# Expert results added to the output rows by accumulating scatters instead of a scratch array and a summing phase

## The chip, the cores and the metric

The kernel runs on one core of a Trainium2 chip. The metric is the device time of one execution in microseconds (us). The profile is one further execution with the hardware profiler on; times inside it count from the start of its span.

## What is computed

The input is 8192 tokens of 128 channels. A graph layer and causal attention come first. Then each token is routed to its two best experts of eight, and this is the part that the change touches. Cut to that part, the reference is:

```python
probs = jax.nn.softmax(flat @ router_w.T, axis=-1)
tp, ti = jax.lax.top_k(probs, TOPK)                      # TOPK = 2, NE = 8
tp = tp / (jnp.sum(tp, axis=-1, keepdims=True) + 1e-09)
weights = jnp.sum(tp[..., None] * jax.nn.one_hot(ti, NE, dtype=flat.dtype), axis=1)
out = jnp.zeros_like(flat)
for e in range(NE):
    hh = jax.nn.silu(flat @ w1[e].T) * (flat @ w3[e].T)
    out = out + weights[:, e:e + 1] * (hh @ w2[e].T)
return x + out.reshape(Bx, Tx, Cx)
```

The result row of a token is thus the residual row plus two weighted expert rows.

## The kernel before

The kernel has three stages, `graph_stage`, `attention_stage` and `expert_stage`, with a barrier of all engines between them. Each stage writes one program per engine by hand, and semaphores order the engines; there is no scheduler. The names in the profile are `PE` (matrix engine), `DVE` (vector), `ACT` (scalar), `POOL` (GpSimd) and `SP` (the engine that only issues transfers).

`attention_stage` ends by leaving the residual of all tokens in on-chip memory (`keep["attended"]`, 128 partitions by 8192) and by scattering every token twice into the DRAM array `scratch_slots`, once per chosen expert, so that each expert's tokens stand together. A slot row holds 128 channels, the routing weight, and a target row number. The target numbers come from POOL's `count_up(target...)`; in the kernel before, token and choice `k` give a row of the scratch array `scratch_parts` (16384 rows: two per token).

`expert_stage` works on groups of 512 slots of one expert. There are `GROUPS` = 39 of them, the greatest number that can occur; groups that are not needed read empty slots, whose target is out of range, so that the scatter writes nothing for them. For each group g:

- SP loads the 512 slot rows into `x_rows` (six buffers).
- PE turns them (`ps_x`), ACT and DVE split them into a high and a low half-precision part (`x_hi`, `x_lo`), PE multiplies by `w1`, `w3` and, one group behind, `w2`; ACT and DVE work on the hidden values between.
- ACT copies the product (`moeT`), PE turns it back (`ps_y`), and DVE, in `scale_parts(g)`, casts the target numbers (`y_index`, L1860) and multiplies by the routing weights (`y_rows`, L1862, semaphore `y_scaled`). `y_rows` and `y_index` have two buffers, so `scale_parts(g)` first waits until the scatter of group g - 2 has landed (`y_scattered`).
- POOL waits for `y_scaled` and issues four indirect transfers of 128 rows each (L1744) into `scratch_parts`.

Behind the last group comes the summing phase. SP waits for all scatters and loads `scratch_parts` in 16 blocks of two parts (L1719, four buffers `parts`), DVE adds the two parts (L1893), POOL adds the residual (L1752), and ACT stores the block to `out` (L1800).

At the start of the stage ACT makes the high halves of the three weight arrays (`w_hi`, L1760), and goes on with `split_tokens(0)`, which writes `x_hi` of the first group (L1766). PE's first product of the stage waits for that.

Of the kernel before, what the change touches and what calls it, by code (L numbers as in the profile page):

```python
# [18 lines left out]
F32 = mybir.dt.float32  # L19
# [6 lines left out]
P = 128  # L26
C = 128
# [633 lines left out]
def attention_stage(nc, NB, dram, keep):  # L661
# [164 lines left out]
    with ExitStack() as ctx:  # L826
# [157 lines left out]
        def _(pool):  # L984
# [72 lines left out]
            for k in range(TOPK):  # L1057
                count_up(target[:, :, :, k], [[BT, NB], [1, SUB]], base=k * N, per_partition=SUB)
            for q in range(PAIRS):
# [545 lines left out]
def expert_stage(nc, NB, dram, keep):  # L1605
# [15 lines left out]
    BUFFERS = 2  # L1621
    PB = 4
    LAST = NB - 1
    TOKEN_SCALE, WEIGHT_SCALE, HIDDEN_SCALE = 2.0 ** 4, 2.0 ** 6, 2.0 ** 4
    with ExitStack() as ctx:
# [26 lines left out]
        y_index = sb("y_index", [P, 2, SUB], mybir.dt.uint32)  # L1652
        parts = sb("parts", [P, PB, TOPK, BT])
        residual = keep["attended"]
# [30 lines left out]
        y_scattered = [sem(f"y_scattered{n}") for n in range(BUFFERS)]  # L1685
        parts_loaded = [sem(f"parts_loaded{n}") for n in range(PB)]
        parts_added = sem("parts_added")
        result_ready = sem("result_ready")
        result_stored = [sem(f"result_stored{n}") for n in range(PB)]
        block = ctx.enter_context(nc.Block())  # L1690
# [4 lines left out]
        @block.sync  # L1695
        def _(sp):
            sp.dma_start(ln2[:], dram["ln2"]).then_inc(small_in, 16)
            for n, name in enumerate(WEIGHTS):
                sp.dma_start(exact[name][:], dram[name]).then_inc(weights_in[n], 16)

            sp.wait_ge(last_scattered, 16 * SUB * TOPK)
            sp.wait_ge(table_ready, 2)
            for g in range(GROUPS):
                if g >= XB:
                    sp.wait_ge(x_turned, g - XB + 1)
                    sp.wait_ge(y_scaled, g - XB + 1)
                start = sp.value_load(start_index[0:1, g:g + 1], min_val=0, max_val=NE * N)
                sp.dma_start(x_rows[:, g % XB], dram["slots"][ds(start, GROUP), :].rearrange("(p s) c -> p s c", s=SUB)
                             ).then_inc(x_loaded[g % XB], 16)

            for n in range(BUFFERS):
                sp.wait_ge(y_scattered[n], 16 * SUB * len(range(n, GROUPS, BUFFERS)))
            for T in range(NB):
                n = T % PB
                if T >= PB:
                    sp.wait_ge(result_stored[n], 16 * (T // PB))
                for k in range(TOPK):
                    at = (k * NB + T) * BT
                    sp.dma_start(parts[:, n, k, :], dram["parts"][at:at + BT, :].rearrange(  # L1719
                        "(p s) c -> p (s c)", s=SUB)).then_inc(parts_loaded[n], 16)  # L1720

        @block.gpsimd
        def _(pool):
# [17 lines left out]
            for g in range(GROUPS):  # L1741
                pool.wait_ge(y_scaled, g + 1)
                for s in range(SUB):
                    pool.indirect_dma_start(  # L1744
                        dram["parts"], bass.IndirectOffsetOnAxis(y_index[:, g % BUFFERS, s:s + 1], 0),
                        y_rows[:, g % BUFFERS, s, :], None, bounds_check=TOPK * N - 1, oob_is_err=False
                    ).then_inc(y_scattered[g % BUFFERS], 16)

            for T in range(NB):
                pool.wait_ge(parts_added, T + 1)  # L1750
                result = parts[:, T % PB, 0, :]
                nc.gpsimd.tensor_tensor(result, result, residual[:, T * BT:(T + 1) * BT], ALU.add).then_inc(result_ready, 1)  # L1752

        @block.scalar
        def _(act):
            act.wait_ge(small_in, 16)
            nc.scalar.mul(ln2_scaled[:], ln2[:], TOKEN_SCALE).then_inc(ln2_ready, 1)
            for n, name in enumerate(WEIGHTS):
                act.wait_ge(weights_in[n], 16)
                nc.scalar.mul(w_hi[name][:], exact[name][:], WEIGHT_SCALE).then_inc(weight_hi_ready, 1)  # L1760
            act.wait_ge(ln2_ready, 1)
            def split_tokens(g):
# [33 lines left out]
            copy_moe(GROUPS - 1)  # L1796

            for T in range(NB):
                act.wait_ge(result_ready, T + 1)
                act.dma_start(dram["out"].rearrange("(b s p) c -> b p s c", s=SUB, p=P)[T], split(parts[:, T % PB, 0, :])  # L1800
                              ).then_inc(result_stored[T % PB], 16)
            for n in range(PB):
                act.wait_ge(result_stored[n], 16 * (NB // PB))

        @block.vector
        def _(dve):
# [82 lines left out]

            for T in range(NB):  # L1890
                n = T % PB
                dve.wait_ge(parts_loaded[n], 16 * TOPK * (T // PB + 1))
                nc.vector.tensor_tensor(parts[:, n, 0, :], parts[:, n, 0, :], parts[:, n, 1, :], ALU.add  # L1893
                                        ).then_inc(parts_added, 1)

        @block.tensor
# [70 lines left out]
def program(nc, N, dram):  # L1967
    NB = N // BT
    for name, shape, dt in (("x1", (NB, P, SUB, C), F32), ("z", (NB, P, SUB, C), F32),
                            ("lower", (NB, P, BT), F32), ("q_hi", (P, N), F16), ("q_lo", (P, N), F16), ("k_hi", (P, N), F16),  # L1970
                            ("slots", (NE * N + GROUP, ROW), F32), ("parts", (TOPK * N, C), F32)):
        dram[name] = nc.dram_tensor(f"scratch_{name}", shape, dt, kind="Internal").ap()
# [70 lines left out]
```

## Time and profile before

| | us |
|---|---|
| median of three timed runs | 3520.46 (3517.39 to 3522.1) |
| profiled execution, its own time | 3524.27 |
| span in the profile | 3522.5 |
| mean granted TensorE clock | 0.943 of full speed |
| start of `expert_stage` in the span | 3164.2 |
| first scatter of results issued | 3214.1 |
| last of the 156 scatters issued | 3471.1 |

The span is shorter than the execution's own time by what lies around it, 1.8 us. The three stages follow each other, so shares over the whole span say little of the last stage; the rows below are of that stage unless their line says otherwise.

### The profile page before, as it was taken

To read this page: it belongs to the slowest core of one execution; us is meant where nothing else is said; L and a number is where in the kernel's file an instruction comes from. 1 tells how busy PE (TensorE), PEld (TensorE's weight loads), DVE (VectorE), ACT (ScalarE), POOL (GpSimd) and SP (SyncE) were. 2 spreads that over 40 slices of the span, in tenths; PEclk is the share of its full clock that TensorE was granted. 3 is DMA by queue.
4 is the path that set the end of the run, shared out by engine and by line. 5 is a ranking of instruction groups with operands and counts; after the bars stand their busy time and mean duration, and the time that the engine had idled before them with its cause. 6 is when DMAs were issued, how large, how long until landed. Compare 5 with 4: busy or idle time off the path is not lost. (4 is left out here: it accounts for less than half of the span.)

```text
span 3522.5 us, 56503 instructions
## 1 busy us (share of the span) xinstructions
PE 3085.2 (88%) x22241; PEld 1353.5 (38%) x22241; DVE 2554.2 (73%) x2736; ACT 1423.8 (40%) x2843; POOL 1728.2 (49%) x1113
## 2 busy tenths in 40 slices
PE   2678889899989987998999999999999999957992
PEld 1334434344434432433433333333333333324661
DVE  8888887675554455779878977877987898616773
ACT  0000000000000003666666666666666666745661
POOL 0000000000321113776888699877699869763665
PEclk9778999999999997999999999999999999988996
DMA  9898876678667944440000000000000000002224
GB/s 376 349 391 366 349 308 267 282 296 302 254 261 292 359 155 167 160 164 13 29 18 18 7 24 17 11 8 7 7 17 18 11 2 17 9 26 93 74 74 154
DMA packets 157501, 506.75 MB, mean 144 GB/s; under 512 B 20081, under 2 KB 66298, under 8 KB 112326
## 3 DMA queue, kind: packets, MB, share of 16 engines
q1 hardware_dynamic: 111400, 448.58, 32.9%
q10 hardware_dynamic: 33024, 31.47, 2.7%
q0 software_dynamic: 12816, 23.11, 2.0%
q8 instruction: 179, 2.93, 0.3%
q14 instruction: 82, 0.67, 0.1%
HBM read 426.31 MB, written 75.37 MB: 142 GB/s over the span
## 5 line engine op out<-in xcount | busy, mean ns | idle before, releaser
L1223 DVE TENSOR_REDUCE unit_max<-ps_max 128x2 f32<-128x1024 f32 (+2 forms) x1088 | 1225.9, 1171 | 297.4 <-PE ps_max L1452 254.1
L998 POOL TENSOR_TENSOR chunk_sum<-chunk_sum,probs 128x1024 f32<-128x1024 f32 x480 | 1132.3, 2359 | 287.8 <-ACT probs L1093 277.1
L1093 ACT ACTIVATE probs<-ps_ring 128x512 f32<-128x512 f32 x2112 | 1089.8, 596 | 440.2 <-PE ps_ring L1471 408.1
L566 PE MATMUL ps_gather<-ring,keep_attended 128*128 128x512 f32 x1688 | 789.8, 625 | 140.1 <-DMA ring<-in_adj 121.4
L1471 PE MATMUL ps_ring<-q_stack,keep_shared 97*128 97x512 f16 x2112 | 673.9, 385 | 27.7 <-ACT probs L1093 22.2
L1486 PE MATMUL ps_acc<-probs,keep_shared 128*32 128x256 f32 (+1 forms) x8448 | 566.8, 386 | 0.0
L566 PEld LDWEIGHTS ps_gather<-ring,keep_attended 128*128 128x128 f32 x1688 | 332.6, 202 | 541.7 <-issue 541.7
L367 DVE TENSOR_TENSOR work<-work,ring 128x2048 f32<-128x2048 f32 x195 | 446.6, 2290 | 34.5 <-DMA ring<-in_adj 30.7
L342 POOL DMA_DIRECT2D scratch_lower<-lower x13 | 7.3, 560 | 805.0 <-ACT lower L484 805.0
L1452 PE MATMUL ps_max<-k_heads,q_heads 32*128 32x512 f16 (+3 forms) x2176 | 276.0, 378 | 69.9 <-DVE unit_max L1223 48.5
L1495 PE MATMUL ps_acc<-probs,keep_ones_heads 128*32 128x256 f32 (+1 forms) x4224 | 327.9, 380 | 0.0
L1471 PEld LDWEIGHTS ps_ring<-q_stack,keep_shared 97*128 97x128 f16 x2112 | 163.5, 98 | 407.7 <-ACT probs L1093 252.0
L1486 PEld LDWEIGHTS ps_acc<-probs,keep_shared 128*32 128x32 f32 x8448 | 222.2, 110 | 244.4 <-issue 121.8
L1744 POOL DMA_INDIRECT scratch_parts<-moe_y_rows,moe_y_index x156 | 168.5, 1080 | 126.5 <-DVE moe_y_rows L1862 87.9
L1452 PEld LDWEIGHTS ps_max<-k_heads,q_heads 32*128 32x128 f16 x2176 | 73.4, 91 | 339.0 <-DVE unit_max L1223 195.5
L350 POOL TENSOR_TENSOR q_lo<-rotated,q_hi 128x512 f16<-128x512 f32 x16 | 18.4, 1151 | 337.0 <-DVEq L460 337.0
L1495 PEld LDWEIGHTS ps_acc<-probs,keep_ones_heads 128*32 128x32 f32 x4224 | 138.0, 111 | 87.7 <-issue 4.1
L566 PE MATMUL ps_gather<-keep_shared,keep_attended 128*128 128x512 f32 x360 | 160.9, 603 | 2.5 <-DVE keep_attended L376 2.5
L367 DVE TENSOR_TENSOR work<-work,keep_shared 128x2048 f32<-128x2048 f32 x45 | 103.1, 2292 | 79.4 <-DMA keep_shared<-in_adj 78.8
L1038 POOL DMA_INDIRECT scratch_slots<-batch_rows,keep_slot_index x120 | 118.8, 990 | 38.1 <-POOL chunk_sum L998 26.0
L473 ACT ACTIVATE root_degree<-ps_degrees 128x4 f32<-128x4 f32 x16 | 2.8, 173 | 324.3 <-PE ps_degrees L593 324.3
L1878 DVE SCALAR_TENSOR_TENSOR moe_hidden<-moe_ps_up,moe_gate 114x512 f32<-114x512 f32 (+1 forms) x117 | 80.9, 691 | 64.0 <-ACT moe_gate L1786 62.8
(243 smaller groups left out, 2667.5 us busy)
## 6 DMA issues: line engine op xcount, KB each, us to landing
ring<-in_adj SPq DMA_DIRECT2D x302, 1024.0 KB, 13.9
keep_shared<-in_adj SPq DMA_DIRECT2D x45, 1024.0 KB, 10.8
scratch_slots<-empty_rows SPq DMA_DIRECT2D x16, 2080.0 KB, 14.3
moe_x_rows<-scratch_slots SPq DMA_DIRECT2D x39, 260.0 KB, 2.7
moe_parts<-scratch_parts SPq DMA_DIRECT2D x32, 256.0 KB, 4.2
x_in<-in_x SPq DMA_DIRECT2D x16, 256.0 KB, 13.3
x_in<-in_x ACTq DMA_DIRECT2D x16, 256.0 KB, 7.5
work<-in_cos ACTq DMA_DIRECT2D x16, 256.0 KB, 4.1
```

What stands on the lines that cost most here:

```text
L367: add = nc.vector.tensor_tensor(total, total, tile_of[g, False], ALU.add)
L566: last = nc.tensor.matmul(bank[:], support[:, s * SUB + c, :], tile_of[g, is_again][:, c * BT:(c + 1) * BT], start=(first and c == 0), sto ...
L998: steps.then(nc.gpsimd.tensor_tensor(totals, totals, weights, ALU.add))
L1038: pool.indirect_dma_start(dram["slots"], bass.IndirectOffsetOnAxis(slot_index[:, at, k:k + 1], 0), rows_of(b)[:, at // SUB, at % SUB, k, : ...
L1093: nc.scalar.activation(probs[:, q % SLOTS, i, kv, :, lo:], halves(bank)[:, :, lo:], ACT.Exp, scale=SCALE).then_inc(ring_read, 1)
L1223: nc.vector.tensor_reduce(unit_max[:, half % 2, heads, s % 2, unit], ps_max[:, base:base + HEADS, at:at + width], AX_X, ALU.max).then_inc( ...
L1452: last = nc.tensor.matmul(ps_max[:, base + n, at:at + width], q_heads[rows, T % 2, s * P:(s + 1) * P], k_heads[rows, G * BT:G * BT + width ...
L1471: last = nc.tensor.matmul(out[:, :, lo:], k_stack[0:STACK, kv, G * BT + j * P:G * BT + (j + 1) * P], q_stack[:, T % QBUF, H, kv * NREP:(kv ...
L1486: nc.tensor.matmul(ps_acc[h * HD:(h + 1) * HD, lo:HALF], values[:, G * SUB + j, kv * HD:(kv + 1) * HD], probs[:, q % SLOTS, i, kv, h % NRE ...
L1495: last = nc.tensor.matmul(ps_acc[at * HD:(at + 1) * HD, HALF + lo:], keep["ones_heads"][:], probs[:, q % SLOTS, i, 1, r, lo:], start=False ...
L1744: pool.indirect_dma_start(dram["parts"], bass.IndirectOffsetOnAxis(y_index[:, g % BUFFERS, s:s + 1], 0), y_rows[:, g % BUFFERS, s, :], Non ...
L1878: nc.vector.scalar_tensor_tensor(out=hidden[0:width, k % HB], in0=ps_up[k % 2][0:width, :], scalar=HIDDEN_SCALE / (TOKEN_SCALE * WEIGHT_SC ...
```

## The change

The scratch array and the summing phase go. ACT stores the residual to `out` block by block, 16 transfers, right behind the weights' high halves. POOL scatters each group's rows straight into `out` with an accumulating transfer (`compute_op=ALU.add`). Two groups can hold the same token, so POOL waits, ahead of a group's first scatter, until the scatters of the group before have landed; ahead of the first group it waits for the stored residual. The target numbers become token numbers, from one index pattern of the same size. What depends on the phase that is gone, its buffers and semaphores, goes too.

```diff
             for k in range(TOPK):
-                count_up(target[:, :, :, k], [[BT, NB], [1, SUB]], base=k * N, per_partition=SUB)
+                count_up(target[:, :, :, k], [[BT, NB], [P, SUB]], base=0, per_partition=1)
...
             for n in range(BUFFERS):
                 sp.wait_ge(y_scattered[n], 16 * SUB * len(range(n, GROUPS, BUFFERS)))
-            for T in range(NB):
-                n = T % PB
-                if T >= PB:
-                    sp.wait_ge(result_stored[n], 16 * (T // PB))
-                for k in range(TOPK):
-                    at = (k * NB + T) * BT
-                    sp.dma_start(parts[:, n, k, :], dram["parts"][at:at + BT, :].rearrange(
-                        "(p s) c -> p (s c)", s=SUB)).then_inc(parts_loaded[n], 16)
...
             for g in range(GROUPS):
                 pool.wait_ge(y_scaled, g + 1)
+                if g == 0:
+                    pool.wait_ge(residual_stored, 16 * NB)
+                else:
+                    pool.wait_ge(y_scattered[(g - 1) % BUFFERS], 16 * SUB * ((g - 1) // BUFFERS + 1))
                 for s in range(SUB):
                     pool.indirect_dma_start(
-                        dram["parts"], bass.IndirectOffsetOnAxis(y_index[:, g % BUFFERS, s:s + 1], 0),
-                        y_rows[:, g % BUFFERS, s, :], None, bounds_check=TOPK * N - 1, oob_is_err=False
+                        dram["out"], bass.IndirectOffsetOnAxis(y_index[:, g % BUFFERS, s:s + 1], 0),
+                        y_rows[:, g % BUFFERS, s, :], None, bounds_check=N - 1, oob_is_err=False,
+                        compute_op=ALU.add
                     ).then_inc(y_scattered[g % BUFFERS], 16)
-
-            for T in range(NB):
-                pool.wait_ge(parts_added, T + 1)
-                result = parts[:, T % PB, 0, :]
-                nc.gpsimd.tensor_tensor(result, result, residual[:, T * BT:(T + 1) * BT], ALU.add).then_inc(result_ready, 1)
...
                 nc.scalar.mul(w_hi[name][:], exact[name][:], WEIGHT_SCALE).then_inc(weight_hi_ready, 1)
+            for T in range(NB):
+                act.dma_start(dram["out"].rearrange("(b s p) c -> b p s c", s=SUB, p=P)[T],
+                              split(residual[:, T * BT:(T + 1) * BT])).then_inc(residual_stored, 16)
             act.wait_ge(ln2_ready, 1)
...
-            for T in range(NB):
-                act.wait_ge(result_ready, T + 1)
-                act.dma_start(dram["out"].rearrange("(b s p) c -> b p s c", s=SUB, p=P)[T], split(parts[:, T % PB, 0, :])
-                              ).then_inc(result_stored[T % PB], 16)
-            for n in range(PB):
-                act.wait_ge(result_stored[n], 16 * (NB // PB))
...
-            for T in range(NB):
-                n = T % PB
-                dve.wait_ge(parts_loaded[n], 16 * TOPK * (T // PB + 1))
-                nc.vector.tensor_tensor(parts[:, n, 0, :], parts[:, n, 0, :], parts[:, n, 1, :], ALU.add
-                                        ).then_inc(parts_added, 1)
```

On POOL, at the first groups of results, the rows of before are these (line, operation, what is written and read, and in brackets the semaphores that the instruction waits for):

```order
L1738 DMA scratch_slots<-keep_rows,keep_slot_index 66048x130 x8
L1744 DMA scratch_parts<-moe_y_rows,moe_y_index 16384x128 [waits moe_y_scaled]
L1744 DMA scratch_parts<-moe_y_rows,moe_y_index 16384x128 x3
L1744 DMA scratch_parts<-moe_y_rows,moe_y_index 16384x128 [waits moe_y_scaled]
L1744 DMA scratch_parts<-moe_y_rows,moe_y_index 16384x128 x3
```

And these are the rows of the changed kernel at the same place:

```order
L1725 DMA scratch_slots<-keep_rows,keep_slot_index 66048x130 x8
L1735 DMA out<-moe_y_rows,moe_y_index 8192x128 [waits moe_residual_stored,moe_y_scaled]
L1735 DMA out<-moe_y_rows,moe_y_index 8192x128 x3
L1735 DMA out<-moe_y_rows,moe_y_index 8192x128 [waits moe_y_scattered0,moe_y_scaled]
L1735 DMA out<-moe_y_rows,moe_y_index 8192x128 x3
```

Each group's first scatter has a second wait now, for the group before it; the number of transfers, four a group, stays.

On ACT, at the start of `expert_stage`, stood:

```order
L1760 ACTIVATE moe_w_hi<-moe_w 128x2728 [waits moe_weights_in1]
L1760 ACTIVATE moe_w_hi<-moe_w 114x3072 [waits moe_weights_in2]
L1766 ACTIVATE moe_x_hi<-moe_ps_x,moe_ln_scaled 128x512 [waits moe_x_turned,moe_ln2_ready]
L1786 ACT_TABLE_LOAD
L1786 ACTIVATE moe_gate<-moe_ps_gate 114x512 [waits moe_up_done] x2
```

There now stands:

```order
L1747 ACTIVATE moe_w_hi<-moe_w 128x2728 [waits moe_weights_in1]
L1747 ACTIVATE moe_w_hi<-moe_w 114x3072 [waits moe_weights_in2]
L1749 DMA out<-keep_attended 128x4x128 x16
L1756 ACTIVATE moe_x_hi<-moe_ps_x,moe_ln_scaled 128x512 [waits moe_x_turned,moe_ln2_ready]
L1776 ACT_TABLE_LOAD
L1776 ACTIVATE moe_gate<-moe_ps_gate 114x512 [waits moe_up_done] x2
```

The sixteen stores, each of 128 partitions by four rows of 128 channels, have moved from the end of ACT's program to a place ahead of the first group's `x_hi`.

## Rows read from the trace of the kernel before

**Rows 1.** Windows: start:end, length, then each engine's busy us, clock, DMA share, GB/s

```profile
core 0: us, PE busy (x) PEld busy (x) DVE busy (x) ACT busy (x) POOL busy (x), PEclk, DMA share, GB/s
3213.40:3473.25 259.85, 244.05 (x1262) 146.84 (x1260) 188.66 (x328) 158.74 (x289) 168.50 (x156) 0.98 0.23 67
3300.00:3400.00 100.00, 100.00 (x521) 60.63 (x520) 77.08 (x134) 64.89 (x119) 64.19 (x60) 1.00 0.26 75
```

**Rows 2.** Timeline of POOL, two groups: start, length, then idle and releaser in brackets

```profile
3430.38 1.39 POOL L1744 DMA_INDIRECT scratch_parts<-moe_y_rows,moe_y_index  x1 [1.50 <-DVE moe_y_rows L1862]
3432.07 0.98 POOL L1744 DMA_INDIRECT scratch_parts<-moe_y_rows,moe_y_index  x1 [0.30 <-issue]
3434.64 0.98 POOL L1744 DMA_INDIRECT scratch_parts<-moe_y_rows,moe_y_index  x1 [0.30 <-issue]
3437.12 1.43 POOL L1744 DMA_INDIRECT scratch_parts<-moe_y_rows,moe_y_index  x1 [1.50 <-DVE moe_y_rows L1862]
...
3460.82 0.98 POOL L1744 DMA_INDIRECT scratch_parts<-moe_y_rows,moe_y_index  x1 [0.30 <-issue]
```

**Rows 3.** Timeline of DVE: first group's rows, one in the middle, last wait

```profile
3212.65 0.68 DVE L1862 TENSOR_TENSOR moe_y_rows<-moe_ps_y,moe_x_rows 128x512 f32<-128x512 f32 x1
...
3428.92 0.68 DVE L1862 TENSOR_TENSOR moe_y_rows<-moe_ps_y,moe_x_rows 128x512 f32<-128x512 f32 x1
...
3463.04 0.17 DVE L1860 CAST moe_y_index<-moe_x_rows 128x4 uint32<-128x4 f32 x1 [4.53 <-DMA scratch_parts<-moe_y_rows,moe_y_index]
```

**Rows 4.** Line 1744: duration in ns (min/median/max), and issue to landing

```profile
L1744 POOL DMA_INDIRECT scratch_parts<-moe_y_rows,moe_y_index x156: 981/982/1482, 3214.1 to 3471.1; - x156
DMA to landing us min/median/max: 2.1/2.3/4.8
```

**Rows 5.** DMA from 3457.5 to 3473: all bytes moved, and the scatters' median landing

```profile
DMA packets 384, 0.03 MB, mean 2 GB/s; under 512 B 368, under 2 KB 372, under 8 KB 384
scratch_parts<-moe_y_rows,moe_y_index POOLq DMA_INDIRECT x12, 2.1
```

**Rows 6.** The chain that ended last, 3465 to 3523: start, length, what

```profile
3471.12 2.12 DMA scratch_parts<-moe_y_rows,moe_y_index
3473.25 0.33 SPq L1719
```

**Rows 7.** Timeline, the last instruction of ACT's queue

```profile
3518.68 0.38 ACTq L1800 DMA_DIRECT2D out<-moe_parts  x1
```

**Rows 8.** Line 1800 (stores), then the landing of line 1719 (loads)

```profile
L1800 ACTq DMA_DIRECT2D out<-moe_parts x16: 378/378/439, 3478.7 to 3518.7; - x16
DMA to landing us min/median/max: 2.2/3.7/6.3
...
DMA to landing us min/median/max: 2.7/4.2/5.8
```

**Rows 9.** DMA from 3473 to 3523, ACT's queue: packets, MB, share of 16 engines

```profile
q10 hardware_dynamic: 8448, 4.20, 28.0%
```

**Rows 10.** Timeline at the start of the expert stage, ACT and PE

```profile
3183.82 2.76 ACT L1760 ACTIVATE moe_w_hi<-moe_w 114x3072 f16<-114x3072 f32 x1 [6.47 <-DMA moe_w<-in_w]
3186.17 1.09 PE L1900 MATMUL moe_ps_x<-keep_ident,moe_x_rows 128*128 128x128 f32 x4 [26.53 <-DMA moe_x_rows<-scratch_slots]
3187.35 0.69 ACT L1766 ACTIVATE moe_x_hi<-moe_ps_x,moe_ln_scaled 128x512 f16<-128x512 f32 x1 [0.76 <-PE moe_ps_x L1900]
```

**Rows 11.** Timeline of SP in the attention stage, second and third of four fills

```profile
1434.87 0.68 SPq L938 DMA_DIRECT2D scratch_slots<-empty_rows  x1
1435.58 5.51 SPq L938 DMA_DIRECT2D scratch_slots<-empty_rows  x1
```

**Rows 12.** Direct transfers issued by POOL, graph stage, ns min/median/max

```profile
L342 POOL DMA_DIRECT2D scratch_lower<-lower x13: 539/539/770, 162.2 to 814.5; - x13
L274 POOL DMA_DIRECT2D keep_shared<-k_hi x56: 496/496/528, 919.9 to 1275.8; - x56
```

**Rows 13.** Windows in the graph stage, columns as in rows 1

```profile
200.00:250.00 50.00, 40.79 (x123) 22.12 (x123) 43.47 (x30) 2.21 (x6) 0.56 (x1) 0.78 1.00 403
1000.00:1050.00 50.00, 44.38 (x121) 20.87 (x120) 23.99 (x46) 2.94 (x8) 7.58 (x13) 0.93 0.94 367
```

More of the change, by code:

```diff
@@ L1621, in expert_stage @@
     BUFFERS = 2
-    PB = 4
     LAST = NB - 1
@@ L1652, in expert_stage @@
         y_index = sb("y_index", [P, 2, SUB], mybir.dt.uint32)
-        parts = sb("parts", [P, PB, TOPK, BT])
         residual = keep["attended"]
@@ L1685, in expert_stage @@
         y_scattered = [sem(f"y_scattered{n}") for n in range(BUFFERS)]
[L1686 to L1689, printed above, removed]
+        residual_stored = sem("residual_stored")
         block = ctx.enter_context(nc.Block())
@@ L1970, in program @@
                             ("lower", (NB, P, BT), F32), ("q_hi", (P, N), F16), ("q_lo", (P, N), F16), ("k_hi", (P, N), F16),
-                            ("slots", (NE * N + GROUP, ROW), F32), ("parts", (TOPK * N, C), F32)):
+                            ("slots", (NE * N + GROUP, ROW), F32)):
         dram[name] = nc.dram_tensor(f"scratch_{name}", shape, dt, kind="Internal").ap()
```

## The prediction

> **What bounds the kernel now.** I read the windows of the last stage first, then POOL's and DVE's timelines there, then the chain that ended last. In steady state PE is busy all of the 100 us between 3300 and 3400 at full clock, while DVE, ACT and POOL have room [rows 1]. So the groups are paced by PE. Their period is read from the starts of two neighbouring groups' first scatters on POOL, 3437.12 - 3430.38 = 6.75 us (rounded up), of which POOL is idle 1.50 us each time, until DVE has the next group's rows [rows 2]. Nobody waits for the scatters' landing until the end of the groups, where DVE meets it once for 4.53 us [rows 3]. The summing phase begins when the last scatter has landed, at 3471.12 + 2.12, and SP starts its first load at 3473.25 [rows 6]; from there to the end of the span at 3522.5 are 49.25 us, in which PE does nothing.
>
> **What is removed.** Those 49.25 us go, except what the end of a program costs behind its last landing. The last store is issued at 3518.68 [rows 7] and stores take 2.2 us at least and 3.7 at the median to land [rows 8], so it lands between 3520.9 and 3522.4 and 0.1 to 1.6 us remain. I take 1. The gain is 48.3 us. DVE's 16 additions and POOL's 16 go with the phase; neither is on another path. The changed index pattern is one instruction of the same size and costs nothing. SP's loop for the groups is as it was; only its loads behind it are gone.
>
> **What is moved: sixteen stores on ACT.** They now stand between the last `w_hi` and the first `x_hi`. The last `w_hi` ends at 3183.82 + 2.76 = 3186.58 and `x_hi` starts at 3187.35, when PE has turned the first rows [rows 10]; so ACT has 0.77 us of slack and everything later is late: `x_hi`, then DVE's `x_lo`, then PE's first product and with it every group. *Lower bound:* an issue takes 0.38 us [rows 8] and I allow 0.04 between two; 16 of them end at 3193.3, and `x_hi` is 5.9 us late. *Upper side:* a queue can be full. Of four fills of 2 MB, 1024 rows each, issued in a row by SP, the second issue took 0.68 us, the third 5.51 [rows 11]: with two in flight the third waited. A store here has 512 rows, so by rows four would be in flight before the fifth waits. The same sixteen stores at the end of the old kernel took 28% of sixteen engines over 50 us, 14.0 us of all engines [rows 9], 0.875 us each. With four in flight the sixteenth is issued when twelve are through: 3186.6 + 1.3 (the fastest landing of 2.2 less 0.9 of data) + 10.5 = 3198.4, 11 us late. I take **11 us** (6 to 13, the latter with two in flight). The stores themselves are done some 4 us later, well before the first scatter wants them, and they share the engines only with five loads of rows that have several us to spare.
>
> **What is added: a wait of each group for the group before.** The wait stands on POOL's queue; behind it are only the scatters. They hold `y_rows`, which DVE needs two groups later; DVE stops there with `hidden` and `x_lo` behind it, and so PE stops. If a group's scatters take longer than 6.75 us from release to landing, the chain of scatters paces the stage, not PE.
>
> How long is one link with plain scatters? DVE's rows end at 3428.92 + 0.68 = 3429.60 [rows 3]; the first scatter starts 0.78 us later and takes 1.39, the other three follow, and the fourth starts at 3434.64 [rows 2], 5.04 us after the release. From there to landing is 2.3 us at the median [rows 4]. So a link is 5.04 + 2.3 = **7.34 us**, already over 6.75. I assume that POOL wakes from a landing as it does from DVE. Scatters that write nothing land after 2.1 (12 scatters with 0.03 MB) [rows 5], so the three empty groups at the end take 7.14 each.
>
> What does accumulating add? The trace has no accumulating transfer, so bounds. *Landing:* nothing at the least. The rows must also be read from DRAM first; the fastest load of 256 KB from DRAM landed after 2.7 us and the fastest store after 2.2 [rows 8], so a read costs 0.5 more of latency. The rows themselves take 2.3 - 2.1 = 0.2 us, and a second stream as much again. I take 0.7. *Issue on POOL:* nothing at the least, since an issue takes 0.98 us whether rows are written or not [rows 2, 5]. With direct transfers, 128 rows took 0.539 us and 32 rows 0.496 [rows 12], 0.4 ns a row; one more read for each of 128 rows would be 0.05 us. At the most, it costs what indexing adds to a direct issue: 0.98 - 0.54 = 0.44 us. I take 0.05, since a further address is nearest to a further row; four issues make 0.2. A link with rows is then 7.34 + 0.7 + 0.2 = **8.24 us**, an empty one 7.34.
>
> The Trainium skill (Collectives: The Full Stack, "The bandwidth ceiling") says that a reduction in the transfer engines is dearer than a copy because it reads two sources on one ring, not because of the add; it halves the rate there. No row here shows such a transfer. By that rule alone the link would be 7.34 + 0.2 = 7.54 us and the time 3516; this is the second rival below.
>
> **The sum.** The first rows are ready at 3212.65 + 0.68 = 3213.33 [rows 3], now 3224.3. Then 36 links of 8.24 (296.6) and 3 of 7.34 (22.0) end at 3542.9, with 1 us behind them 3543.9. Against the span of before: the groups' scatters took 3473.25 - 3213.33 = 259.9 us and take 318.6 (+58.7), the start is 11 later, the phase gives back 48.3: **+21.4 us**. The profiled execution's own time was 3524.27, 3.8 us over the median of 3520.46; against that median I predict **3542 us**, 0.6% slower. The span would not change with links of 7.69 us. Faster or slower by 0.2% (7 us, about what timing this kernel can tell from no change) needs links under 7.51 or over 7.87.
>
> **Rivals.**
> 1. *Landing as cheap as a plain write* (the end on the other side): links of 7.34 to 7.5. With 7.34 the end is 3224.3 + 264.2 + 21.4 + 1 = 3510.9, 11.6 us faster, **3509 us**; with the lower bound for ACT too 3505.8, or 3504 as a median. For it: DVE was released 2.2 us after the issue at 3460.82 [rows 2, 3], so most of a landing does not depend on the data. Against it: the read. It decides below 7.51 us a link.
> 2. *Only the traffic doubles*: 7.54 us, end 3518.1, **3516 us**, no change that can be told.
> 3. *A dear issue*: 0.44 more on each scatter, so 7.34 + 0.7 + 1.76 = 9.8 and empty links 8.9; the end is 3224.3 + 352.8 + 26.7 + 1 = 3604.8, **3603 us**. For it: indexing costs about that. Against: the count of rows costs almost nothing.
> 4. *The rows of a scatter are read one after the other.* Each of sixteen engines has 8 rows, and 8 times 0.5 us are 4 us for a scatter instead of 1.3; a link would be near 18 us and the time near **3900 us**. Nothing in the trace speaks for it but that no such transfer is seen.
> 5. *PE's clock.* With links of 8.24 PE works 6.75 of them, 82%, the share in the graph stage (40.79 of 50 us), where the mean clock was 0.78 in one stretch and 0.93 in another at 89% [rows 13]. At 0.78 a group needs 8.65 us of PE, which then paces: 0.41 times 36 is 15 us more, **3557 us**.
>
> **Chances.** The forecast, links of 7.87 to 9 us: 0.42. Rival 1: 0.18. Rival 2 with its neighbours, 7.51 to 7.87: 0.15. Rival 3: 0.15; rival 4: 0.06; rival 5: 0.04. Faster is rival 1, 0.18; same is rival 2, 0.15; slower the rest, 0.67. The range leaves out rival 4 and the cheaper part of rival 1: 3506 to 3603. The forecast's own is 3527 to 3570.
>
> **What would show it.** POOL's first scatter of a group starts about 0.8 us after a landing, no longer after DVE's `y_rows`; the starts of first scatters are 8.2 us apart; the scatters' median landing is 3.0 us, their duration near 1.03. PE is busy some 82% in the middle of the stage, and DVE waits at the cast of `y_index` for the scatter in every group. `x_hi` of the first group starts near 3198, with ACT issuing stores before it. The end follows the last landing by about 1 us, with no phase behind it. The prediction is wrong if landing or issue of an accumulating scatter differ by a few tenths of a us from what I took (0.1 us on each link is 4 us), or if the issue on ACT does not block.

## The result and the profile after

| | before, beside it | after |
|---|---|---|
| median of 4 runs each | 3521.28 us (3517.39 to 3523.87) | 3629.34 us (3625.45 to 3632.8) |
| ratio, 95% interval | | 1.0308 (1.029 to 1.0325) |
| span of the profiled execution | 3522.5 us | 3624.4 us |

The change makes the kernel 3.1% slower, 108 us. The forecast was 3542 us, with 3603 us as the end of its range; the direction was forecast, the size was not.

The windows of the last stage, in the columns of [rows 1], show at once that PE no longer paces it:

```profile
3300.00:3400.00 100.00, 73.53 (x338) 41.81 (x335) 48.13 (x86) 43.86 (x78) 65.77 (x39) 0.93 0.34 46
3400.00:3500.00 100.00, 82.29 (x342) 45.85 (x343) 50.21 (x88) 43.26 (x77) 67.70 (x40) 0.83 0.36 50
```

Where 60 scatters were issued in 100 us before, there are 39 and 40 now, and yet POOL is as busy as it was: each of them takes longer. The lower clock of the second window makes PE's work longer, but PE has 18 us to spare there, and the waits from 3200 to the end (engine, line and what it waited for: us in total, times, longest) say who was waited for:

```profile
DVE moe_y_index L1843 <- DMA out<-moe_y_rows,moe_y_index: 153.4, 36, 8.9
POOL out L1735 <- DMA out<-moe_y_rows,moe_y_index: 90.8, 36, 3.4
PE moe_ps_y L1877 <- DVE moe_y_rows L1845: 89.2, 33, 6.7
```

POOL waits for the group before it to land in 36 of 39 groups, DVE for the buffer of those scatters, and PE for DVE. The chain of the forecast is there, from the scatters back to PE. POOL's timeline shows one link of it, from the first scatter of a group to the first of the next, to be laid beside [rows 2]:

```profile
3389.27 1.56 POOL L1735 DMA_INDIRECT out<-moe_y_rows,moe_y_index  x1 [2.36 <-DMA out<-moe_y_rows,moe_y_index]
3391.13 1.99 POOL L1735 DMA_INDIRECT out<-moe_y_rows,moe_y_index  x1 [0.30 <-issue]
3393.42 1.98 POOL L1735 DMA_INDIRECT out<-moe_y_rows,moe_y_index  x1 [0.30 <-issue]
3395.70 1.55 POOL L1735 DMA_INDIRECT out<-moe_y_rows,moe_y_index  x1 [0.30 <-issue]
3399.87 1.56 POOL L1735 DMA_INDIRECT out<-moe_y_rows,moe_y_index  x1 [2.61 <-DMA out<-moe_y_rows,moe_y_index]
```

From the first scatter of this group to the first of the next are 10.60 us. Over the stage the first scatter of the first group starts at 3220.99 and that of the last at 3613.38, 38 links later: 10.33 us a link, where 8.24 were forecast. The line as a whole, beside [rows 4] (duration in ns, min/median/max; then what POOL was idle for ahead of it, and the landings):

```profile
L1735 POOL DMA_INDIRECT out<-moe_y_rows,moe_y_index x156: 1550/1558/2073, 3221.0 to 3619.0; - x156
...
  DMA out<-moe_y_rows,moe_y_index: 90.8, 36
...
DMA to landing us min/median/max: 2.7/3.6/5.1
```

An issue that took 0.98 us takes 1.55 at the least. On the page, the same group and POOL's DMA queue (packets, MB, share of 16 engines), and behind them that queue on the page of before:

```profile
L1735 POOL DMA_INDIRECT out<-moe_y_rows,moe_y_index x156 | 266.6, 1709 | 181.1 <-DMA out<-moe_y_rows,moe_y_index 90.8
q0 software_dynamic: 30288, 23.12, 3.8%
...
q0 software_dynamic: 12816, 23.11, 2.0%
```

The mean is 1.709 us, so four issues take 6.84 us. The queue moves the same bytes as before in 17472 more packets, 112 more for each of the 156 scatters. Twelve empty scatters had 384 packets before [rows 5], 32 each; now a scatter has 144, which is sixteen and one for each of its 128 rows. The start of the stage, beside [rows 10], first ACT and PE, then the line of ACT's stores with their landings:

```profile
3179.54 2.76 ACT L1747 ACTIVATE moe_w_hi<-moe_w 114x3072 f16<-114x3072 f32 x1 [6.45 <-DMA moe_w<-in_w]
3182.05 1.09 PE L1877 MATMUL moe_ps_x<-keep_ident,moe_x_rows 128*128 128x128 f32 x4 [26.85 <-DMA moe_x_rows<-scratch_slots]
3194.36 0.69 ACT L1756 ACTIVATE moe_x_hi<-moe_ps_x,moe_ln_scaled 128x512 f16<-128x512 f32 x1 [12.06 <-issue]
...
L1749 ACTq DMA_DIRECT2D out<-keep_attended x16: 395/730/1577, 3179.5 to 3193.6; - x16
DMA to landing us min/median/max: 3.2/5.6/6.5
```

PE has turned the first rows at 3183.14 and ACT starts `x_hi` 11.2 us later (it was 0.09 behind PE before). From 3179.5 on, and so already ahead of PE's turn, ACT's queue issues the sixteen stores, at 0.73 us each by the median and 1.58 at the most; the last issue begins at 3193.6.

### The profile page after: what moved, and what is told of

Read it like the earlier page. It is cut to its first block and busy times, and to the rows that moved or that the text cites. A ratio compares the mean times of both kernels' runs of the same rounds, so it can differ in the third digit from the quotient of the medians.

```text
span 3624.4 us, 56476 instructions
## 1 busy us (share of the span) xinstructions
PE 3127.9 (86%) x22241; PEld 1367.0 (38%) x22241; DVE 2535.8 (70%) x2720; ACT 1427.5 (39%) x2843; POOL 1805.8 (50%) x1097
## 5 line engine op out<-in xcount | busy, mean ns | idle before, releaser
L1735 POOL DMA_INDIRECT out<-moe_y_rows,moe_y_index x156 | 266.6, 1709 | 181.1 <-DMA out<-moe_y_rows,moe_y_index 90.8
L1776 ACT ACTIVATE moe_gate<-moe_ps_gate 114x512 f32<-114x512 f32 (+1 forms) x117 | 69.9, 597 | 137.5 <-PE moe_ps_up L1883 137.5
```

Source lines behind the costliest of these rows:

```text
L1735: pool.indirect_dma_start(dram["out"], bass.IndirectOffsetOnAxis(y_index[:, g % BUFFERS, s:s + 1], 0), y_rows[:, g % BUFFERS, s, :], None, ...
L1776: nc.scalar.activation(gate[0:width, k % 2], ps_gate[k % 2][0:width, :], ACT.Silu, scale=1.0 / (TOKEN_SCALE * WEIGHT_SCALE)).then_inc(gate ...
```

## The experiments

The theory that these rows suggest is called A below: an accumulating scatter is dearer for POOL to *issue*, by 0.57 us, and by more when something else on the chip holds it up (a long issue, some 2.0 us), and four issues stand in each link. Its rival B puts the loss on the new wait between the groups; further ones are stated where they are tested. All edits are to the changed kernel but the last. Only two of the runs were timed in several rounds, those with an interval; the others are one execution each, with its profile, and are read for their links and issues more than for their times.

**1. Scatters that do not accumulate, everything else as changed.**

```diff
-                        y_rows[:, g % BUFFERS, s, :], None, bounds_check=N - 1, oob_is_err=False,
-                        compute_op=ALU.add
+                        y_rows[:, g % BUFFERS, s, :], None, bounds_check=N - 1, oob_is_err=False
```

> The changed kernel with the accumulating taken out: the scatters write plainly into the output, with the wait for the group before kept (the output then lacks the residual and one expert where a token's rows are overwritten). Theory A, the accumulating scatter is dear to issue (1.56 us and more instead of 0.98): issues go back to 0.98 with about one of 1.39 in a group, a link from group to group is 7.3 us instead of 10.3, and the time is 3629 - 116 = 3513 us. Theory B, the wait itself (waking POOL and the landing) makes the long link: only the later landing goes, 0.4 us a link, and the time is about 3612. Theory C, the output array is dearer to write than the scratch array: issues stay at 1.56 and the time at 3629.

It ran in 3510.06 us, beside 3523.85 for the kernel before on the same chip. POOL's timeline of this kernel over a link, and its line:

```profile
3390.70 0.98 POOL L1735 DMA_INDIRECT out<-moe_y_rows,moe_y_index  x1 [2.12 <-DMA out<-moe_y_rows,moe_y_index]
...
3394.56 0.98 POOL L1735 DMA_INDIRECT out<-moe_y_rows,moe_y_index  x1 [0.30 <-issue]
3397.65 0.98 POOL L1735 DMA_INDIRECT out<-moe_y_rows,moe_y_index  x1 [2.12 <-DMA out<-moe_y_rows,moe_y_index]
...
L1735 POOL DMA_INDIRECT out<-moe_y_rows,moe_y_index x156: 980/982/1500, 3223.8 to 3503.5; - x156
```

The wait is there in every link, and a link is (3499.61 - 3223.80) / 38 = 7.26 us; the forecast's sum for plain scatters was 7.34, and its time for them (rival 1) 3509. So the wait, the stores on ACT and the lost phase together are as forecast, and the miss lies in accumulating: it costs 119 us against this run, where the forecast had 3542 - 3509 = 33. In a link it is 10.33 - 7.26 = 3.07 us: the issues of a group take 6.84 instead of 4.02 (2.82), and the idle time ahead of the first one, by the mean of all 38 links, is 2.56 instead of 2.27 (0.29; the rest is rounding and one longer gap of the plain kernel). Theory B would have left 3612, and theory C is out: with the same target array the issues are back at 0.98.

**2. Accumulating scatters without the wait.** Each expert rank of a token gets a row of its own in a scratch array again, so that no two groups meet.

```diff
-                count_up(target[:, :, :, k], [[BT, NB], [P, SUB]], base=0, per_partition=1)
+                count_up(target[:, :, :, k], [[BT, NB], [P, SUB]], base=k * N, per_partition=1)
...
-                else:
-                    pool.wait_ge(y_scattered[(g - 1) % BUFFERS], 16 * SUB * ((g - 1) // BUFFERS + 1))
...
-                        dram["out"], bass.IndirectOffsetOnAxis(y_index[:, g % BUFFERS, s:s + 1], 0),
-                        y_rows[:, g % BUFFERS, s, :], None, bounds_check=N - 1, oob_is_err=False,
+                        dram["parts"], bass.IndirectOffsetOnAxis(y_index[:, g % BUFFERS, s:s + 1], 0),
+                        y_rows[:, g % BUFFERS, s, :], None, bounds_check=TOPK * N - 1, oob_is_err=False,
...
-                            ("slots", (NE * N + GROUP, ROW), F32)):
+                            ("slots", (NE * N + GROUP, ROW), F32), ("parts", (TOPK * N, C), F32)):
```

> The changed kernel with the wait for the group before taken out; so that nothing is added to the same row at the same time, the scatters add into a scratch array with a row of its own for each token and choice, which nobody reads (the output is the residual alone). Theory A: POOL's issues alone pace the groups, four of 1.56, four gaps of 0.30 and 0.6 for long ones are 8.1 us a group, PE still waits, and the time is 3629 - 83 = 3546 us. Theory B: without the wait the groups are back at 6.75 us and the time is 3629 - 136 = 3493.

It took 3527.86 us, with a link of 7.61 us: nearer to A's 3546 than to B's 3493. POOL's timeline at a boundary of two groups, and the line:

```profile
3396.97 1.55 POOL L1733 DMA_INDIRECT scratch_parts<-moe_y_rows,moe_y_index  x1 [0.30 <-issue]
3398.83 1.56 POOL L1733 DMA_INDIRECT scratch_parts<-moe_y_rows,moe_y_index  x1 [0.30 <-DVE moe_y_rows L1843]
...
L1733 POOL DMA_INDIRECT scratch_parts<-moe_y_rows,moe_y_index x156: 1554/1558/2083, 3226.1 to 3520.7; - x156
```

POOL goes from group to group without a pause: four issues and four gaps of 0.30 us are 7.6 us and are the whole link, longer than the 6.75 that PE needs [rows 2]. DVE still waited 35 times for a buffer (79.0 us). So the dear issue alone makes POOL the pace. Without the wait between groups and without the 49 us of the old phase, though with the 11 us that the stores cost the start, this kernel is still not faster than before (3523.85 on the same chip). A had taken more long issues than came: 13 of 156, where the changed kernel has 56.

**3. Fewer rows in some of the scatters.** Two of a group's four scatters take 64 and 32 of their 128 rows.

```diff
+    ROWS = (128, 64, 32, 128)
...
-                        dram["out"], bass.IndirectOffsetOnAxis(y_index[:, g % BUFFERS, s:s + 1], 0),
-                        y_rows[:, g % BUFFERS, s, :], None, bounds_check=N - 1, oob_is_err=False,
+                        dram["out"], bass.IndirectOffsetOnAxis(y_index[0:ROWS[s], g % BUFFERS, s:s + 1], 0),
+                        y_rows[0:ROWS[s], g % BUFFERS, s, :], None, bounds_check=N - 1, oob_is_err=False,
```

> The changed kernel in which the four scatters of a group take 128, 64, 32 and 128 rows (the other rows are left out). If each row that is added to costs POOL time at the issue, the second and the third take clearly less than 1.56 us, near 1.1 and 0.9, and the time falls by some 40 us or more. If the 0.57 us over a plain scatter are a fixed price of an accumulating transfer, all four take 1.56 and the time falls by less than 10 us.

3612.07 us. POOL's timeline of a group without long issues:

```profile
3590.04 1.57 POOL L1736 DMA_INDIRECT out<-moe_y_rows,moe_y_index  x1 [2.31 <-DMA out<-moe_y_rows,moe_y_index]
3591.91 1.43 POOL L1736 DMA_INDIRECT out<-moe_y_rows,moe_y_index  x1 [0.30 <-issue]
3593.64 1.34 POOL L1736 DMA_INDIRECT out<-moe_y_rows,moe_y_index  x1 [0.30 <-issue]
3595.28 1.57 POOL L1736 DMA_INDIRECT out<-moe_y_rows,moe_y_index  x1 [0.30 <-issue]
```

Neither expectation was met: 128, 64 and 32 rows take 1.57, 1.43 and 1.34 us, so a row costs 2.2 to 2.8 ns, and drawn back to no row at all some 1.26 us are left, an estimate from these three sizes. Four scatters of an empty group have 416 packets here, four times sixteen and one for each of the 352 rows, so a packet a row holds for the shorter ones too.

**4. The same with plain scatters**, to split the extra.

```diff
+    ROWS = (128, 64, 32, 128)
...
-                        y_rows[:, g % BUFFERS, s, :], None, bounds_check=N - 1, oob_is_err=False,
-                        compute_op=ALU.add
+                        y_rows[0:ROWS[s], g % BUFFERS, s, :], None, bounds_check=N - 1, oob_is_err=False
```

> The kernel with plain scatters into the output and the wait (the first experiment), with 128, 64, 32 and 128 rows in the four scatters of a group. With accumulating, 128, 64 and 32 rows took 1.57, 1.43 and 1.34 us. If accumulating has a fixed price of 0.58 us, the plain issues take 0.98, 0.85 and 0.76. If its price is by the row, the plain issues fall by no more than direct transfers do, 0.4 ns a row, and stay at 0.98, 0.95 and 0.94. Time 3510, less 5 at most.

3489.55 us, and in the same view as above:

```profile
3480.24 0.99 POOL L1736 DMA_INDIRECT out<-moe_y_rows,moe_y_index  x1 [1.98 <-DMA out<-moe_y_rows,moe_y_index]
3481.53 0.91 POOL L1736 DMA_INDIRECT out<-moe_y_rows,moe_y_index  x1 [0.30 <-issue]
3482.75 0.88 POOL L1736 DMA_INDIRECT out<-moe_y_rows,moe_y_index  x1 [0.31 <-issue]
3483.93 0.99 POOL L1736 DMA_INDIRECT out<-moe_y_rows,moe_y_index  x1 [0.30 <-issue]
```

Neither expectation for the plain issues was met either: they fall by 1.1 ns a row, between the two. Accumulating adds 0.58, 0.52 and 0.46 us for 128, 64 and 32 rows. A line through these gives 1.2 ns a row, 0.15 us for 128 of them, and some 0.43 us whatever the rows. By this estimate three quarters of the extra do not depend on the rows, although the packets grow by one a row. The time fell by 20 us where 5 at most were expected: a link is 6.98 us instead of 7.26, 11 us in all, and this execution started its scatters 8.6 us sooner.

**5. DVE's subtraction with one on-chip input from elsewhere.** The long issues of 1.98 us lie where DVE runs line 1836, which reads two arrays of on-chip memory (last section). Here it reads PE's accumulator memory (PSUM) for one of them, which takes the low half from another difference, and PE must wait for DVE before it writes that bank again.

```diff
-                nc.vector.tensor_tensor(hidden_lo[0:width, at], hidden[0:width, at], hidden_hi[0:width, at],
+                nc.vector.tensor_tensor(hidden_lo[0:width, at], ps_up[k % 2][0:width, :], hidden_hi[0:width, at],
...
-                    pe.wait_ge(hidden_done, k - 1)
+                    pe.wait_ge(hidden_lo_ready, k - 1)
```

> The changed kernel in which DVE's subtraction for the low half of the hidden values reads its first input from PE's accumulator memory instead of on-chip memory (the low half is then wrong; PE waits for this subtraction before it writes that bank again). Theory P, the issues of about 2.0 us instead of 1.56 are those at whose start DVE runs this subtraction with two inputs from on-chip memory: nearly all issues are 1.56, a link is 0.6 us shorter, the time is about 24 us less, 3605. Rival: the long issues have another cause and stay at a third of all; the time changes by less than 8 us.

The line, with what POOL was idle for ahead of it, and one row of the waits from 3230 to 3480:

```profile
L1735 POOL DMA_INDIRECT out<-moe_y_rows,moe_y_index x156: 1549/1557/1618, 3236.1 to 3648.3; - x156
...
  DVE moe_y_rows L1845: 178.4, 35
...
PE moe_ps_gate L1881 <- DVE moe_hidden_lo L1836: 80.8, 70, 1.4
```

What was expected of the issues came: none is longer than 1.62, although at the start of 68 of them the subtraction is running. What was expected of the time did not: 3655.44 us, slower. PE now waits 70 times for that subtraction, and POOL waits for DVE's rows, 35 times, where it waited for landings. The edit brought a wait of its own, so its time tells nothing of the long issues' price.

**6. The low half set to zero**, which leaves PE's waits as they are and takes the two inputs away. The product loses its low half.

```diff
-                nc.vector.tensor_tensor(hidden_lo[0:width, at], hidden[0:width, at], hidden_hi[0:width, at],
-                                        ALU.subtract).then_inc(hidden_lo_ready, 1)
+                nc.vector.memset(hidden_lo[0:width, at], 0.0).then_inc(hidden_lo_ready, 1)
```

> The changed kernel in which DVE writes zeros for the low half of the hidden values (the product loses that part) instead of subtracting two arrays of on-chip memory; PE's waits are as in the changed kernel. If the issues of 2.0 us come from that subtraction at their start, nearly all issues are 1.56, a link is 0.6 us shorter and the time 23 us less, 3606. If they have another cause, about a third stays at 2.0 and the time within 6 us of 3629.

3595.39 us, and again no long issue:

```profile
L1735 POOL DMA_INDIRECT out<-moe_y_rows,moe_y_index x156: 1549/1557/1617, 3213.8 to 3588.2; - x156
```

A link is 9.71 us, 0.62 less than in the changed kernel, 23.6 us over 38 links. (This execution came to the stage some 7 us earlier, 3213.8 against 3221.0, which is the rest of the difference to what was expected.) So of the 3.07 us that accumulating costs a link, about 0.5 to 0.6 come from issues that DVE lengthens, and four times 0.57 from the issues themselves; what is left is the landing.

**7. The stores on SP's queue**, behind the six loads that the first groups need.

```diff
             for g in range(GROUPS):
+                if g == XB:
+                    for T in range(NB):
+                        sp.dma_start(dram["out"].rearrange("(b s p) c -> b p s c", s=SUB, p=P)[T],
+                                     split(residual[:, T * BT:(T + 1) * BT])).then_inc(residual_stored, 16)
...
-            for T in range(NB):
-                act.dma_start(dram["out"].rearrange("(b s p) c -> b p s c", s=SUB, p=P)[T],
-                              split(residual[:, T * BT:(T + 1) * BT])).then_inc(residual_stored, 16)
```

> The changed kernel with the sixteen residual stores issued by SP behind the first six loads of token rows, instead of by ACT ahead of the first high halves of the tokens. If the stores cost the start 11 us, the first high halves start 0.1 us behind PE's turn again, everything is 11 us earlier, and the time is 3629 - 11 = 3618 us. If the stores only shift work that has to wait for the same transfers anyway (the loads of rows share the engines with them), less than 4 us come back.

Its median is 3613.12 us (3610.38 to 3615.4, 4 runs), 1.0256 of before (1.0231 to 1.028), against 1.0308 (1.029 to 1.0325): the intervals do not meet, and the difference is 0.0052 x 3522 = 18 us. PE and ACT at the start of the stage, then the lines of SP's stores and of POOL's scatters:

```profile
3182.97 1.09 PE L1878 MATMUL moe_ps_x<-keep_ident,moe_x_rows 128*128 128x128 f32 x4 [26.81 <-DMA moe_x_rows<-scratch_slots]
3184.15 0.69 ACT L1757 ACTIVATE moe_x_hi<-moe_ps_x,moe_ln_scaled 128x512 f16<-128x512 f32 x1 [0.92 <-PE moe_ps_x L1878]
...
L1701 SPq DMA_DIRECT2D out<-keep_attended x16: 379/648/906, 3186.0 to 3196.7; - x16
L1739 POOL DMA_INDIRECT out<-moe_y_rows,moe_y_index x156: 1554/1558/2062, 3210.9 to 3607.7; - x156
```

`x_hi` is 0.09 us behind PE's turn again. In the two traces the first scatter starts at 3210.9 instead of 3221.0 although PE's turn is 0.9 later: 11 us, as forecast. Links are the same (10.30), and the two profiled spans differ by 3624.4 - 3613.1 = 11.3 us. The two intervals leave anything from 4 to 33 us, so that the 18 us of the medians do not contradict the 11.

**8. The kernel before with eight buffers in the summing phase** instead of four. The trace of before leaves the transfers' engines room in that phase, so a part of its 49 us might be had without accumulating.

```diff
-    PB = 4
+    PB = 8
```

> The kernel before, with eight instead of four buffers in the summing phase, so that SP's loads wait less for stores. The phase takes 49 us, in which the transfers take 81% of the sixteen engines (53% and 28% of 50 us, 40.5 us of work). If the buffers hold the loads up, the phase falls to some 42 us and the time to 3521 - 7 = 3514; if the transfer engines are the limit with rows of 512 B and 2 KB mixed, nothing changes (within 2 us).

3513.69 us (3508.0 to 3516.11, 10 runs), 0.9972 of before (0.9961 to 0.9983): 8 us faster than before on the same chip, as expected of buffers that hold the loads up, and so faster than both kernels. The phase in windows, first of the kernel before, then of this one (columns as in [rows 1]):

```profile
3473.25:3522.50 49.25, 0.00 (x0) 0.00 (x0) 12.77 (x16) 0.00 (x0) 20.60 (x16) 0.50 0.82 256
```

```profile
3473.07:3512.70 39.63, 0.00 (x0) 0.00 (x0) 15.32 (x16) 0.00 (x0) 21.73 (x16) 0.50 0.92 318
```

The phase is 9.6 us shorter, the transfers' engines are busy 92% of it instead of 82.

The links and issues of the kernels, each a mean over 38 links (first scatters of the first and the last group) and 39 groups; as long counts an issue that takes over 0.15 us more than the usual 0.98 or 1.56:

| kernel | link, us | four issues, us | long issues, of 156 |
|---|---|---|---|
| before | 6.66 | 4.31 | 36 |
| 1 plain, with wait | 7.26 | 4.02 | 7 |
| 2 accumulating, no wait | 7.61 | 6.38 | 13 |
| 6 accumulating, low half zero | 9.71 | 6.22 | 0 |
| 7 accumulating, stores on SP | 10.30 | 6.81 | 54 |
| after | 10.33 | 6.84 | 56 |

## Why the prediction was wrong in size

**The end of the program**, right within 2 us. The last issue starts at 3618.98, and empty scatters land 2.7 us after their start, at 3621.7; 2.7 us remain to the end of the span, where I took 1. There is no phase behind it.

**The stores on ACT**, right in what they cost, 11.2 us late where 11 were taken, and in part by luck. That the issue would block was the open point; the median of 0.73 us for a store, twice the 0.38 of [rows 8], and experiment 7 settle it. But the terms were off and offset each other. The stores began with the last `w_hi` and not behind it, 2.75 us sooner than I let them. From the first issue to `x_hi` they took 14.8 us, where I had 3198.4 - 3186.6 = 11.8. Some six were in flight and not four, by an estimate from 5.6 us to a landing and an issue every 0.94. And the loads of rows, whose share I left out, took part of the transfers' engines: from 3179.5 to 3200 the stores' queue had 68.1% of them and the loads' 24.2%. On SP, behind those loads, the same stores went out in 10.7 us from the first issue to the last, against 14.1 here; that the loads alone make this difference is not shown, since the queue is another too.

**The wait and its chain**, right: a wait of POOL in 36 groups, DVE and PE behind it, release of POOL 0.8 us after a landing. (A detail of the kernel before was misread: DVE met a landing there twice, for 0.95 and 4.53 us, and not once.) One landing can be read in the chain of work that ended last (start, length, what):

```profile
3590.76 3.34 DMA out<-moe_y_rows,moe_y_index
```

It ends at 3594.10 and POOL starts at 3594.93, 0.83 later. The sum for plain scatters, 7.34, measured 7.26.

**The landing**, over-sized. I took 0.7 us more for the read of the rows; between the plain and the accumulating kernel POOL's idle time ahead of a group grows by 0.29 us by the mean, and by 0.5 between links like those shown (2.12 and 2.61). For empty scatters nothing is added behind the issue: 2.7 less 1.56 is 1.1 us, and 2.1 less 0.98 was the same [rows 5]. The Trainium skill's rule that a reduction costs its two reads and not its add (Collectives: The Full Stack, "The bandwidth ceiling") gave the landing 0.2, so that the measured 0.3 to 0.5 lies between it and my 0.7. But it speaks of the transfer engines alone, and they are not where the time went.

**The issue on POOL**, the step that failed: "one more read for each of 128 rows would be 0.05 us. At the most, it costs what indexing adds to a direct issue: 0.98 - 0.54 = 0.44 us. I take 0.05, since a further address is nearest to a further row." Measured are 0.57 on every scatter, over the upper bound, and with the long ones the mean is 1.709 us where the forecast's four issues made 4.53 / 4 = 1.13. Both halves of the argument were off. The rows' share is 1.2 ns a row and not 0.4 (experiments 3 and 4); and most of the extra is no matter of rows, so that a price read from the count of rows could not hold it. The rows of before had no instruction that could show a fixed price of another kind of transfer; 0.44 was therefore not a bound, only the one comparison at hand. Right among the rivals was the third, the dear issue, with 9.8 us a link where 10.33 were measured; I gave it 0.15. That its link came so near is in part luck, since its landing was too long and its issue too short.

**The sum with what was measured.** The groups' scatters took from 3220.2 (the first rows ready) to 3621.7, 401.5 us, and I had 318.6. Of these 82.9 us, four issues at 6.84 instead of 4.53 are 2.31 a link and 90 in 39 links; the shorter idle time ahead of a group (2.56 instead of 2.80) takes back 9.1 in 38 links; the three empty links, which I had 0.9 cheaper and which pay the same issue, are 2.7. That is 83.7, near enough. From the forecast end of 3543.9 the span follows: 82.9 more for the scatters, 1.7 more at the end, and 4.1 less because this execution came to the stage earlier (PE's turn ended at 3183.14 and not 3187.26), 3624.4.

**The other rivals.** Rows read one after the other did not come: links would be near 18. PE's clock did fall, to 0.83 in the second window, and costs nothing there: POOL's links are the same length in both windows (39 and 40 scatters).

What stays open is what POOL does in the fixed 0.43 us or so of an accumulating issue; no run here looks into it.

## What to carry to other kernels

Before a phase is folded into the transfers of another one, count the issues: a price of half a microsecond on each of 156 serial issues was worth more than the 49 us phase that it replaced. When the profile has no instruction of the new kind, a bound taken from its nearest kin is an estimate and no bound, and the range should reach past it by its own size, above all where the issuing engine will be the pace. A phase that is to be removed should first be asked for its slack: four more buffers gave a fifth of it back for on-chip memory alone.

## What the runs showed of the hardware

**An indirect issue on POOL takes up to 0.51 us longer, mostly 0.43, if DVE is reading two on-chip arrays when it starts.** DVE's timeline in the changed kernel, over the link shown at first:

```profile
3391.01 0.68 DVE L1836 TENSOR_TENSOR moe_hidden_lo<-moe_hidden,moe_hidden_hi 114x512 f16<-114x512 f32 x1
...
3393.29 0.68 DVE L1836 TENSOR_TENSOR moe_hidden_lo<-moe_hidden,moe_hidden_hi 114x512 f16<-114x512 f32 x1
```

They start 0.12 and 0.13 us ahead of POOL's issues at 3391.13 and 3393.42 and reach 0.56 and 0.55 us into them, and these two take 1.99 and 1.98; the two others of the group, with no subtraction at their start, take 1.56 and 1.55. All 56 long issues of this trace have a subtraction running at their start, and what they take goes by what is left of it: 1.66 us with 0.23 left, 1.78 with 0.35, 1.98 with 0.56, 2.07 with 0.65. That is 0.13 us less than what is left, on top of 1.56, as if the issue waited for the end of the subtraction 0.13 us after its own start. Where a subtraction ends 0.07 us or less after an issue's start, or starts 0.01 us ahead of it or later, the issue is not longer. Plain issues show the same step, 1.39 for 0.98 [rows 2]. Without an operation of two on-chip inputs on DVE (experiments 5 and 6) there is none among 156. How many issues are long goes by how DVE's work falls against POOL's: 36 of 156 before, 56 in the changed kernel, 13 when that does not wait. One landing releases POOL and DVE there, which may bring their work together; but plain scatters with the same wait had 7, so that this is not shown.

The Trainium skill (SBUF — State Buffer, "Who interferes with whom") says that a VectorE instruction with two inputs in on-chip memory contends with a GpSimd instruction that reads there, over a shared read interface, that the shared ports are an exclusive lock, and that the order of issue decides who is held up. The trace agrees, by what is left of the subtraction, for an issue that reads its row numbers on the chip; that it waits at this interface is argued from that section of the Trainium skill and from experiments 5 and 6, and no row shows the interface itself. The same section infers that such a two-input operation does not hold up GpSimd's writing of transfers; the measured 1.98 against 1.55 says that the issue as a whole is held up, and it is what counts here.

**An accumulating scatter is cut into a packet a row** (144 packets instead of 32 for 128 rows, sixteen and one a row), empty ones too, and yet its landing behind the end of the issue is 0 to 0.5 us later only.

**ACT issues transfers while its last operation is still running:** its first store is issued at 3179.55, 0.01 us after the start of `w_hi`, which runs until 3182.30. The forecast had let them begin at its end.
